# Supertiles of six tiles in a two-layer graph kernel, and TensorE's table product ahead of a step's weights

## What is computed

```python
h = jnp.maximum(_layernorm(x), 0.0)
x = x + segment_sum(h[src] * edge_weight[:, None], dst)           # layer 0
h = jnp.maximum(_layernorm(x), 0.0)                               # layer 1
w = (relu(edge_feat @ W1 + b1) @ W2 + b2).reshape(e, 4, 8, 8)     # w_000, w_011, w_101, w_110
s_e, v_e = h[:, :8][src], h[:, 8:].reshape(n, 8, 3)[src]
m0 = ALPHA * (einsum('ei,eio->eo', s_e * sh0, w_000) + C110 * einsum('eim,em,eio->eo', v_e, sh1, w_110))
m1 = ALPHA * (einsum('ei,em,eio->eom', s_e, sh1, w_011) + einsum('eim,eio->eom', v_e * sh0, w_101))
x = x + segment_sum(concat(m0, m1), dst) + SI_SCALE * (h by si_w0 and si_w1)
```

## Time and profile before

| | us |
|---|---|
| median of 3 runs | 6679.0 |
| lowest, highest | 6676.37, 6683.61 |
| the profiled execution, span | 6674.1 |

### The profile page before, as it was taken

How to read it: one execution, slowest core, us unless ns; L and a number is a source line. 1 busy time by engine, 2 the same in 40 slices (tenths; PEclk the granted TensorE clock), 3 DMA queues, 4 the chain that set the end, 5 groups by cost and what they waited for, 6 DMA issues and landing times.

```text
span 6674.1 us, 156533 instructions
## 1 busy us (share of the span) xinstructions
PE 6489.0 (97%) x40552; PEld 4418.8 (66%) x40552; DVE 5619.0 (84%) x14128; ACT 2966.1 (44%) x12673; POOL 4878.7 (73%) x5214
## 2 busy tenths in 40 slices
PE   6999999999999999979999999999999999999998
PEld 5888888888888888855555555555555555555554
DVE  7887777777777777769999999999999999999997
ACT  2222222222222222245555555555555555555555
POOL 5777777777777777767777777777777777777775
PEclk9999999999999999979999999999999999999998
DMA  4111111111111111111111111111111111111111
GB/s 106 34 32 33 32 32 32 32 32 33 32 32 32 32 32 32 33 38 36 34 33 34 35 34 33 34 35 34 33 34 35 34 33 34 35 34 33 34 34 32
DMA packets 331940, 235.18 MB, mean 35 GB/s; under 512 B 109833, under 2 KB 328281, under 8 KB 331405
## 3 DMA queue, kind: packets, MB, share of 16 engines
q0 software_dynamic: 163424, 84.00, 9.0%
q1 hardware_dynamic: 167500, 147.69, 8.2%
q10 hardware_dynamic: 990, 3.21, 0.2%
HBM read 229.28 MB, written 5.23 MB: 35 GB/s over the span
## 4 chain that ended last, share of the span: by engine, by line
PE 62%; POOL 26%; issue 10%; DVE 1%; POOLq 1%; DMA 1%; SPq 0%; ACT 0%; DVEq 0%; ACTq 0%
POOL z L457 26%; PE hp_ps L821 15%; PE sc_ps L795 12%; PE w_ps L780 10%; PE w_ps L770 7%; PE w_ps L701 6%; PE w_ps L789 5%; PE w_ps L776 3%; PE w_ps L786 2%; PE w_ps L800 1%; PE w_ps L711 0%; POOLq L454 0%; PE hp_ps L711 0%; DMA x_sb<-in_x 0%; DMA z<-h_table,idx 0%
## 5 line engine op out<-in xcount | busy, mean ns | idle before, releaser
L457 POOL DMA_INDIRECT z<-h_table,idx x5107 | 4834.7, 947 | 1711.4 <-issue 1576.3
L701 PE MATMUL w_ps<-parts,pick 128*128 128x448 f32 x11662 | 2537.2, 371 | 59.2 <-DVE pick L1014 57.4
L701 PEld LDWEIGHTS w_ps<-parts,pick 128*128 128x128 f32 x11662 | 2143.9, 188 | 245.1 <-issue 57.4
L559 ACT ACTIVATE z<-z,squares 128x32 f32<-128x32 f32 x3125 | 736.5, 309 | 2064.4 <-DMA z<-h_table,idx 1945.9
L821 PE MATMUL hp_ps<-parts,pick 128*128 128x448 f32 x4340 | 1044.7, 380 | 0.0
L610 ACT ACTIVATE hid<-w_ps,b_sb 128x320 f32<-128x320 f32 x625 | 329.5, 527 | 1525.3 <-PE w_ps L770 1525.2
L821 PEld LDWEIGHTS hp_ps<-parts,pick 128*128 128x128 f32 x4340 | 766.7, 188 | 251.9 <-issue 205.9
L1014 DVE TENSOR_TENSOR pick<-sc_ps,feat 128x896 fp32r<-128x896 f32 x833 | 889.1, 1088 | 48.8 <-issue 43.6
L795 PE MATMUL sc_ps<-prod,onehot 128*32 128x344 f32 x6250 | 842.0, 463 | 4.3 <-DVE reduced_sb L1144 4.3
L1174 DVE TENSOR_TENSOR prod<-w_ps,coef 128x192 f32<-128x192 f32 x1250 | 808.7, 647 | 0.3 <-ACT coef L617 0.3
L654 ACT ACTIVATE near<-iota_sb,rel_sb 128x32 f32<-128x32 f32 x3125 | 722.4, 309 | 0.0
(11 more groups left out here) (92 smaller groups left out, 5078.8 us busy)
## 6 DMA issues: line engine op xcount, KB each, us to landing
z<-h_table,idx POOLq DMA_INDIRECT x5107, 2.4
feat<-key_table SPq DMA_DIRECT2D x311, 192.0 KB
ft_sh_sb<-in_ft_sh SPq DMA_DIRECT2D x313, 180.0 KB
feat<-key_table SPq DMA_DIRECT2D x210, 64.0 KB
h_table<-big SPq DMA_DIRECT2D x10, 280.0 KB
rel_sb<-in_dst_t SPq DMA_DIRECT2D x1, 1562.5 KB, 12.0
idx_all<-in_src_t SPq DMA_DIRECT2D x1, 1532.5 KB, 8.3
squares<-in_ew_t SPq DMA_DIRECT2D x1, 1532.5 KB, 11.7
```

Source lines behind the costliest of these rows:

```text
L457: pool.indirect_dma_start(z[:, r, u, :], None, rows, bass.IndirectOffsetOnAxis(ap=idx[:, r, u:u + 1], axis=0)).then_inc(z_in[r], 16)
L559: last = nc.scalar.activation(z[:, r, u, :], z[:, r, u, :], ACT.Copy, scale=ew_all[:, bass.ds(n * G + u, 1)])
L701: mm = pe.matmul(fold_ps[:, pick_banks[k], 0:NC * D], pick[:, k, blk, :], parts[:, t, :, blk, :], start=(blk == 0 and t == 0), stop=(blk = ...
```

## The change

A supertile has six tiles (768 edges). The edges are padded to whole rings: 522 supertiles, 896 edges of weight zero among them. In layer 0 three supertiles have five table products in five banks (EXTRA = 2 of the three have two) and thirteen gathers. The sums of layer 0 have two banks in place of three, and VectorE takes a supertile's sums five steps late in place of six. In layer 1 five of six supertiles (`on_pe`) have a table product, and its 14 matmuls stand in one piece behind the next supertile's `hidden` and ahead of the step's biases and weights; the fold and the window sums follow the weights. The weights of six tiles are three pairs, each of one product in the upper and one in the lower half of the array's rows; the third pair has a bank of its own that is used by every supertile. The window sums of the tiles 5 and 6 are cut in halves of 172 columns over the four column places. VectorE takes the pair's two tiles first; its group selection stands behind the reduction of `t011`. ScalarE prepares one supertile ahead in one piece. Some SBUF tiles of layer 1 move into a part of `squares`. SyncE loads layer 1's keys in two lots of a ring (three rows and two).

```diff
-G = 5
+G = 6
-SLOTS = PERIOD + 1
+EXTRA = 2
+SLOTS = PERIOD + EXTRA
+PE1 = R1 - 1
+PAIR = 2
     def gathered_by_pool(r):
-        return GT - 1 if r % PERIOD == PERIOD - 1 else GT
+        return GT - 1 if r % PERIOD < EXTRA else GT
     def first_pick(b, r):
-        return b * (R0 // PERIOD * SLOTS) + r + r // PERIOD
+        return b * (R0 // PERIOD * SLOTS) + r // PERIOD * SLOTS + 2 * (r % PERIOD)
     def on_pe(r):
-        return r % 2 == 0
+        return r < PE1
...
-        total0_ps = [fold_ps[0:D, PEG, 0:WIN], fold_ps[0:D, PEG + 1, 0:WIN], hp_ps[0:D, 0:WIN]]
+        total0_ps = [fold_ps[0:D, PEG + 1, 0:WIN], hp_ps[0:D, 0:WIN]]
-        pick_banks = (0, 1, 2, PEG + 2)
+        pick_banks = (0, 1, 2, PEG, PEG + 2)
...
 # ScalarE, layer 1: prepare(n + 1) in step n
+                def prepare(m, bv, v, t):
+                    act.wait_ge(hidpre_ready, m + 1)
+                    if t is None or t >= 2:
+                        act.wait_ge(wts_ready, m - 1)
+                    relu_hidden(v % 2).then_inc(hid_ready, 1)
...
 # TensorE, layer 0
-                    if s is None or s >= 7:
-                        pe.wait_ge(acc0_done, n - 6)
+                    if s is None or s >= 6:
+                        pe.wait_ge(acc0_done, n - 5)
...
 # TensorE, layer 1
+            def weights(n, q, turn):
+                low, high = halves
+                tile_weights(q, 2, turn, halves[turn], 2, False).then_inc(half_ready, 1)
+                if turn:
+                    tile_weights(q, 0, 0, low, 0, False)
+                    tile_weights(q, 1, 0, high, 0, False)
+                    tile_weights(q, 0, 1, low, 1, True)
+                    tile_weights(q, 1, 1, high, 1, True)
...
+                pe.wait_ge(half_ready, n + 1)
+                return tile_weights(q, 2, 1 - turn, halves[1 - turn], 2, True)
             def window_sums(r, v):
+                half = TILE // 2
+                for k in range(4):
+                    pe.matmul(sums_ps[k * WIN:(k + 1) * WIN, :], onehot[:, r, k, :], prod[:, v, k], start=True, stop=False)
+                for k in range(4):
+                    u, cols = 4 + k // 2, slice(k % 2 * half, (k % 2 + 1) * half)
+                    mm = pe.matmul(sums_ps[k * WIN:(k + 1) * WIN, cols], onehot[:, r, u, :], prod[:, v, u, cols],
+                                   start=False, stop=True)
...
+                if s is None or s < S:
+                    if s is None or s >= 1:
+                        pe.wait_ge(last_wts_used, n)
+                    bias(q, 2, halves[q])
+                    if s is None or s + 1 < S:
+                        if r % 2:
+                            pe.wait_ge(ft_in[(r + 1) % R1 // 2], (b + (r + 1) // R1 + 1) * 16)
+                        pe.wait_ge(hid_ready, n + 1)
+                        hidden((r + 1) % R1).then_inc(hidpre_ready, 1)
+                bt, t = before(b, r, R1, -2)
+                if on_pe(t) and (s is None or R1 <= s + 2 < S):
+                    i = nth(bt, t)
...
+                    pe.wait_ge(pick1_ready, i + 1)
+                    if s is None or s + 2 > R1:
+                        pe.wait_ge(group1_step, i * 2)
+                    for blk in range(GB):
                         for p in range(2):
                             mm = pe.matmul(picked_ps, pick[:, t, blk, :], parts[:, p, :, blk, :],
                                            start=(blk == 0 and p == 0), stop=(blk == GB - 1 and p == 1))
+                    mm.then_inc(picked1, 1)
                 if s is None or s < S:
                     if s is None or s >= 2:
                         pe.wait_ge(wts_used, n - 1)
-                    weights(q)
+                    bias(q, q, halves[q])
+                    bias(q, 1 - q, halves[1 - q])
+                    pe.wait_ge(hid_ready, n + 1)
+                    weights(n, q, q).then_inc(wts_ready, 1)
+                if s is None or s >= 3:
+                    pe.wait_ge(sum1_reduced, n - 2)
+                    if s is None or s >= 4:
+                        pe.wait_ge(acc1_done, n - 3)
+                    fold_sums((r - 3) % 2).then_inc(sum1_folded, 1)
+                if s is None or 2 <= s <= S + 1:
+                    v = (r - 2) % R1
+                    pe.wait_ge(msg1_ready, n - 1)
+                    pe.wait_ge(hot1_ready, n - 1)
+                    window_sums(v, v % 3).then_inc(sum1_ready, 1)
...
 # VectorE, layer 0
-                    base = first_column(n - 6)
-                    dve.wait_ge(sum0_ready, n - 5)
+                    base = first_column(n - 5)
+                    dve.wait_ge(sum0_ready, n - 4)
...
 # VectorE, layer 1: products, then reduce
-                scalar_products(last_wts_ps, last_tile)
+                scalar_products(last_wts_ps, last_tiles)
                 dve.wait_ge(coef_ready, n + 1)
-                vector_rows(last_wts_ps, last_tile)
-                take()
+                vector_rows(last_wts_ps, last_tiles)
                 step(2)
-                scalar_rows(last_wts_ps, last_tile).then_inc(last_wts_used, 1)
+                scalar_rows(last_wts_ps, last_tiles).then_inc(last_wts_used, 1)
                 scalar_products(wts_ps[q], first_tiles).then_inc(prod_step, 1)
                 vector_rows(wts_ps[q], first_tiles)
+                place()
                 scalar_rows(wts_ps[q], first_tiles).then_inc(wts_used, 1)
-                select()
                 step(3)
                 nc.vector.tensor_reduce(t011[:], p011[:], AX, ALU.add
                                         ).then_inc(prod_step, 1)
+                select()
                 reduce()
...
-                i, v, done = nth(b, r, 3), (r + 3) % R1, nth(b, r, 3) * 2
+                bt, v = before(b, r, R1, -2)
+                i = nth(bt, v)
...
+                selects = on_pe((r + 2) % R1) and (s is None or R1 <= s + 2 < S)
                 def reduce():
+                    if s is None or s >= 3:
+                        dve.wait_ge(sum1_folded, n - 2)
                     if s is None or 2 <= s <= S + 1:
                         dve.wait_ge(sum1_ready, n - 1)
+                    if s is None or s >= 3:
+                        take_sums(n - 3, None if s is None else s - 3, base[0], acc1_done, total1_ps)
+                    if on_pe((r + 4) % R1) and (s is None or R1 <= s + 4 < S):
+                        make_pick1(b, r, s)
+                    if s is None or 2 <= s <= S + 1:
                         reduce_sums(q).then_inc(sum1_reduced, 1)
                     if selects:
                         sum_groups1(b, r)
```

More of the change, by code:

```diff
@@ L638, in edge_rows @@
-                if s is None or 1 <= s <= S:
-                    scale()
+                    if t is None or t >= 2:
+                        act.wait_ge(wts_used, m - 1)
+                    if on_pe(v) and (t is None or t >= R1):
+                        act.wait_ge(selected1, nth(bv, v) + 1)
+                    scale_rows(m, v, v % 2)
+                    if t is None or t >= 1:
+                        act.wait_ge(hot1_ready, m)
+                    for u in range(G):
+                        last = nc.scalar.activation(near[:, u, :], iota_sb[:], ACT.Abs, scale=-1.0,
+                                                    bias=rel_sb[:, bass.ds(m * G + u, 1)])
@@ L640, in edge_rows @@
+                    last.then_inc(near_ready, 1)
+                    act.wait_ge(near_ready, m + 1)
+                    if t is None or t >= R1:
+                        act.wait_ge(sum1_ready, m - R1 + 1)
+                    nc.scalar.activation(onehot[:, v], near, ACT.Relu, scale=-1.0, bias=one_sb[:]
+                                         ).then_inc(hot1_ready, 1)
                 if s == 0:
-                    act.wait_ge(hidpre_ready, 1)
-                    relu_hidden(0).then_inc(hid_ready, 1)
+                    prepare(0, 0, 0, 0)
@@ L643, in edge_rows @@
                 if s is None or s + 1 < S:
[L644 to L655, removed]
@@ L656, in edge_rows @@
-                last.then_inc(near_ready, 1)
-                act.wait_ge(near_ready, n)
-                nc.scalar.activation(onehot[:, v], near[:], ACT.Relu, scale=-1.0, bias=one_sb[:]).then_inc(hot1_ready, 1)
+                    prepare(n + 1, *before(b, r, R1, -1), None if s is None else s + 1)
+                if s is None or s + R1 < S:
+                    copy_indices(n + R1, r, idx1_ready)
                 if s == 1:
@@ L770, in hidden @@
                 return pe.matmul(hidden_ps, w1_sb[rows, :], ft_of(r), start=True, stop=True)
[L772 to L776, removed]
-                for j in range(2):
-                    for k in range(2):
-                        half = slice(k * HID, (k + 1) * HID)
-                        mm = pe.matmul(w_ps[:, q, k, j * WN:(j + 1) * WN], hid[half, q, j * P:(j + 1) * P], w2_sb[half, :],
-                                       start=False, stop=(j == 1))
-                return mm
@@ new lines, in weight_bank, with bias, tile_weights @@
```

(19 more changed lines are left out.)

248 lines of the change are left out of this document (95 added, 153 removed).

## The result

The changed kernel takes 8,189.7 us (median of 4, 8,187.0 to 8,192.1) against 6,677.8 before: a ratio of 1.226, 95% interval 1.2245 to 1.2281. It is slower, inside the predicted range of 7,400 to 8,350 us and 280 us above the predicted 7,910.

The account below looks back on a forecast made before the run. A closed loop of waits between TensorE and VectorE would bound layer 1; 6,679 + 80 (layer 0) + 742 (layer 1) + 5 (preparation) = 7,506 us, with 410 for the clock 7,916, stated as 7,910; range 7,400 to 8,350 us.

Parts of the forecast that it names:

- The loop in layer 1: Weights, VectorE's products, group multiplication, table product, next weights: 4.10 + 4.92 + 0.2 = 9.2 us a step.
- The step from 2 to 3: Layer 1, where step 3 has no table product or group selection: VectorE's own work, 6.95 us.
- that from 3 to 4: Layer 1 step running through the third bank: bank free, hidden, product, biases and weights, hand-overs, 7.0 us.
- the ring: Six steps of layer 1: 4 x 9.2 + 6.95 + 7.0 = 50.75 us; layer 1 742 us longer.
- The clock: TensorE's granted clock in layer 1 falls at six in ten of the idle gaps: 4.8 us a ring, 410 us.
- the upper bound given: Layer 1's clock falling at all five gaps of a ring, 1.6 us each over 86 rings: 690 us.
- the one-in-three: Share of layer 0's three gaps in the earlier trace after which the clock fell; the forecast took six in ten.
- Layer 0: TensorE stalls 0.56 us once a period, waiting for VectorE's reduction: 16.92 us a period, 80 us more in all.
- That the clock holds: Rival for layer 1: the clock survives the gaps, as behind two of three before; 7,506 us; chance 0.25.
- that it stays low for long: Rival: the clock falls at every gap and stays low beyond the next product; over 8,200 us; chance 0.12.
- That VectorE bounds layer 1: Rival: the product's wait costs nothing, VectorE's own steps bound layer 1; ring 39.4 us, whole 6,533; chance 0.05.
- That row pairs run one after another: Rival for layer 1: paired row halves don't overlap, 1.6 us more a loop; 8,200 us at full clock; chance 0.04.

Follow-up runs that it names:

- the experiment: Changed kernel with only layer 0 edited: VectorE takes a window's sums six steps late again, the two banks kept; 8,045.4 us, 144 less than the changed kernel.

## Why the prediction was right, and where it was off

**The loop in layer 1** was right in its place, its members and its size: predicted 9.2 us at full clock, 8.9 in the kernel with the filled gap, VectorE's wait 2.25 against 1.99. The terms that were a little long are the third row pair and the restart of biases and weights: 1.88 us and a hand-over of 0.1, where the trace has 1.73 from the first bias to VectorE's start. That one wait makes the loop is shown twice, by cutting it on TensorE's side and on VectorE's. The step from 2 to 3 was predicted at 6.95 and is 6.86; that from 3 to 4, predicted at 7.0, is 9.53 with the clock and by the estimate above 6.8 without. So the ring is some 49.3 us at full clock where 50.75 stood, some 120 us less in all.

**The clock** was named as the open term, its mechanism was right and its size too small. I took it to fall in six gaps of ten, 410 us; it falls in all five of a ring. By the rings that is 8.7 us a ring, an estimate as said above, and some 745 us over 86 rings; filling brought back 604 of it and cost 1.58 x 86 = 136 in the step from 3 to 4. A fall costs about 1.7 us here, and the upper bound given, 690 us for all five at 1.6 us, was nearly right. The share of gaps was the term that failed: the earlier trace rows told little of it. Outside that list the trace before has two gaps of 2.5 us ahead of sums at the ends of the two loops (2,904.8 and 6,635.1 us), and the clock fell behind both.

Right ahead of the gap TensorE runs `hidden` alone, and the earlier trace rows had shown that such work doesn't bring the clock back; that sentence deserved more weight than the one-in-three. That the work ahead of a gap makes the difference is not shown by a run, though: no experiment keeps the gap and changes that work alone. The advice of the Trainium skill (TensorE: Matmul & The Clock Gate, "Why this matters for your kernels") is to avoid idle gaps longer than these between bursts of matmuls; taken as the limit, it would have left the clock at 1.0. The trace has it at 0.57 behind a gap of 1.90 us, and here the measurement decides.

**Layer 0** was right in its cause, short in its size: 0.56 us a period predicted, 0.59 and 0.98 by turns measured, 17.24 us a period in place of 16.92. The missing part is VectorE's 0.43 us at the ring's end, which the working left out. The wait costs 144 us by the experiment, where 0.56 x 174 = 97 stood; against the kernel before, layer 0 is 147 us longer where 80 stood. Without the wait the period is 16.40, predicted 16.36. The preparation ahead of layer 0 took 9.6 us more (first table product at 67.0, before at 57.4), not 5.

**By layers**, from first table product of layer 0 to first `hidden` of layer 1, and from there to the last fold: 2,914 and 3,669 us before, 3,061 and 5,033 after. The differences, 147 and 1,363, stand against 80 and 742 + 410 = 1,152. So the 280 us between forecast and result are some 335 of clock and 67 of layer 0 too few, and some 120 of loop too many: by luck, the error in the loop hid a third of that in the clock.

**The rivals.** That the clock holds falls with the windows; that it stays low for long falls too, since it is back at 1.00 before the weights in each step. That VectorE bounds layer 1 is false of this kernel and true of the one with the product behind the weights: the prediction's 39.4 us for that ring is 38.86, its 6,533 us for the whole 6,549, where the shorter ring and the longer layer 0 nearly cancel. That row pairs run one after another is false: twelve passes take 1.46 us.

## What to carry to other kernels

Draw the waits of two in-order queues as a loop before placing a block: an operation that waits for what another engine makes from this step's output must not stand ahead of the next step's output in its own queue. Moving either end, the block behind the weights or the multiplication ahead of its wait, gave back 1,641 and 1,388 us, the clock's part included. A gap on TensorE costs more than its length when the clock falls in it; where a gap can't be removed, products that nobody reads may be cheaper than idling.

## What was not expected of the hardware

In 85 rings of the changed kernel the clock fell with every gap of 1.87 to 2.17 us, 425 of 425, while of three gaps of 1.76 to 1.94 us between table products and sums in the kernel before two cost nothing.

Shorter gaps can be enough, and the length of a single one doesn't decide. In the step without a product the kernel with the earlier multiplication has gaps of 1.32 and 1.11 us with only the fold and the window sums between them, and the clock fell in 34 of 85 rings; with the product behind the weights they are 0.9 us (in 63 of the rings) and 1.11 us (in all), and it fell in 22 of 85. With the product at the end of the step there are again gaps of 1.11 and 1.32 us, but `hidden` and the weights lie between them, and it fell in none of 85. What tells these cases apart was not tested.

And constant products in these gaps, seven ahead of each table product and four ahead of the fold, made the kernel 604 us faster at the same order.
